# Window attention and 3x3 convolution on one core: the loops of both stages written out in line

## Chip, core and metric

The kernel runs on one core of one Trainium2 chip. The metric is the device time of one execution in microseconds. Three runs of the kernel before gave a median of 4224.94 us (4220.99 to 4227.97). The profile comes from one more execution, which took 4226.05 us by the same clock.

## What is computed

The input is x, of shape (2, 128, 256, 256) in float32. Two residual layers follow each other:

```
# layer 0: windows of 8x8 queries over 12x12 keys, 4 heads of 32
x = x + W_out * attention(W_qkv * group_norm(x))   # with relative positions and a fixed mask
# layer 1: 3x3 convolution, 128 to 128 channels, of the tile-masked input
x = x + conv3x3(tile_mask(group_norm(x))) + bias
```

The fixed mask lets each query see the keys of one parity class only. So the kernel splits the picture into four classes by the parity of row and column (PAR = 4) and runs attention with 16 queries against 36 keys.

## The kernel before, in words

Channels lie on the 128 partitions, and the 512 rows of both pictures stand one below the other. There are four phases. The first loads x, takes its statistics (VectorE) and scales the weights. A short step turns the sums into the mean and deviation of each group. The third phase is the attention stage, which writes x1 to HBM. After a second statistics step and a small table of tile masks comes the convolution stage.

**Attention.** A unit is 8 rows by half a width of 128 columns, so there are UNITS = 128. Each unit has four groups (GROUPS = 4) of four windows. In each group TensorE issues, in this order: the scores (L421, 16 products of 54 columns), half of the transposes (L401), projections q and k of a unit ahead (L386, L389), v (L434), attention times v (L451), the other half of the transposes (L401) and the output projection (L462). float32 products appear in the trace as two passes, each with its own weight load. VectorE gathers the queries of the next unit into a block layout (`sb_qb`, L541, four copies in groups 1 and 3), adds positions to the scores (L521), takes maxima and sums (L502, L506, L527), adds the output to x1 (L495) and takes the statistics of x1 (L533, L548). ScalarE evicts PSUM (L562, L566, L581, L588, L593, L599), takes the exponential (L576) and normalises the input (L610, L616). GpSimd has four kinds of elementwise operation (L635, L642, L651, L658). SyncE only issues DMAs (L348 on). The engines are coupled by counting semaphores: each instruction waits for the count that its unit and group need.

**The loop of units.** Each engine has a `body(u, s, slot, on)`, which emits what that engine does in unit u. `units(eng, body)` (L330) drives it. Units -3 to 5 are written out with constants; units 6 to 121 run in a hardware loop (L333) of 29 turns (TURNS) with four units in a turn; units 122 to 131 are written out again. A call where u is a constant emits constant waits and addresses. In the loop u is an expression of the loop's register, so that waits and the few moving addresses are computed by register instructions (`need`, L74 to L78, `settled`, L69). At the end of a turn each engine adds to its register, compares and branches back to the head of its own loop.

**Convolution.** A strip is 8 rows of 256 columns, and there are CSTRIPS = 64. The rows are combined in fours on GpSimd (L900), split into two float16 parts (L835 on ScalarE, L882 on VectorE), and 72 products of 512 columns per strip run on TensorE (L808). VectorE adds the four results (L872). ScalarE also normalises a strip ahead (L827) and starts the output with x1 plus bias (L848). `strips(eng, body)` (L753) is the same kind of driver: strips -4 to 3 in line, a loop (L756) of 14 turns (CTURNS) of four strips, the rest in line.

Of the kernel before, what the change touches and what calls it, by code (L numbers as in the profile page):

```python
# [32 lines left out]
UNITS = 2 * STRIPS  # L33
# [18 lines left out]
CSTRIPS = ROWS // CROWS  # L52
# [28 lines left out]
def conv_preact_program(nc, x_in, wqkv_in, wout_in, rel_in, wconv_in, bias_in, ident_in, gsum_in,  # L81
                        shift_in, edge_in, x1_dram, out):
    with ExitStack() as ctx:
# [205 lines left out]
        with ExitStack() as pb:  # L289
# [33 lines left out]

            FIRST, LOOP = 6, 4
            TURNS = (UNITS - 3 - FIRST) // LOOP
            GT = UNITS * GROUPS

            def units(eng, body):  # L330
                for u in range(-3, FIRST):
                    body(u, u // 2, u % 4, lambda v, top: 0 <= v < top)
                with eng.Fori(0, TURNS) as i:  # L333
                    for c in range(LOOP):
                        body(i * LOOP + (FIRST + c), i * (LOOP // 2) + (FIRST + c) // 2, (FIRST + c) % 4,
                             lambda v, top: True)
                for u in range(FIRST + LOOP * TURNS, UNITS + 4):
                    body(u, u // 2, u % 4, lambda v, top: 0 <= v < top)

            def z_at(slot, p, off, dims):  # L340
# [5 lines left out]
            @block.sync  # L346
            def _(sp):
                def body(u, s, slot, on):  # L348
                    h = slot % 2
                    if on(u + 3, UNITS):  # L350

                        row = settled(sp, (s + (h + 3) // 2) * WS)
                        need(sp, sem["zf_done"], u + 2)
                        r = (slot + 3) % 2
                        sp.dma_start(view(xb, 0, 128, r * ZR * LC, [[LC, ZR], [1, LC]]),
                                     x_in[:, bass.ds(row, ZR),
                                          (UW - PAD) * r:(UW - PAD) * r + LC]).then_inc(x_loaded[r], 16)
                    if on(u - 3, UNITS):
                        row = settled(sp, (s - 1 - (1 - h)) * WS + 1)
                        sp.wait_ge(sem["x1_done"], (u - 2) * PAR)  # L360
                        sp.dma_start(x1_dram[:, bass.ds(row, WS), UW * (1 - h):UW * (1 - h) + UW],
                                     view(x1, 0, 128, (1 - h) * WS * UW, [[UW, WS], [1, UW]])
                                     ).then_inc(sem["x1_stored"], 16)
                    if on(u - 1, UNITS):

                        row = settled(sp, (s + (h - 1) // 2) * WS + PAD)
                        done = settled(sp, (u - 2) * 16)
                        need(sp, sem["x1_read"], done)
                        need(sp, sem["x1_stored"], done)
                        r = (slot + 3) % 2  # L370
                        sp.dma_start(view(x1, 0, 128, r * WS * UW, [[UW, WS], [1, UW]]),
                                     x_in[:, bass.ds(row, WS),
                                          UW * r:UW * r + UW]).then_inc(xr_loaded[r], 16)
                units(sp, body)
                sp.wait_ge(sem["x1_stored"], UNITS * 16)

            @block.tensor
            def _(pe):
# [87 lines left out]
                def QF_BEFORE(n):  # L466
                    return min(n + PAR + 2, UNITS * PAR) if isinstance(n, int) else n + PAR + 2
                units(pe, body)

            @block.vector  # L470
            def _(dve):
# [6 lines left out]
                def body(u, s, slot, on):  # L478
                    h = slot % 2
                    for g in range(GROUPS):  # L480
# [64 lines left out]
                        if g == 2 and on(u - 3, UNITS):  # L545

                            for t, op in ((tmax, ALU.max), (tmin, ALU.min)):
                                last = dve.tensor_reduce(t[:, bass.ds((u - 3) * 4, 4)],  # L548
                                                  view(x1, 0, 128, (1 - h) * WS * UW, [[TILE, 4], [UW, WS], [1, TILE]]),
                                                  AX.XY, op)  # L550
                            last.then_inc(sem["x1_read"], 16)
                units(dve, body)

            @block.scalar
# [176 lines left out]
        with ExitStack() as pc:  # L731
# [3 lines left out]
            XR = 4  # L735
# [12 lines left out]
            ADDS = (2, 4, 5, 6)  # L748
            NADD = ADDS[-1]

            CFIRST, CTURNS = 4, 14

            def strips(eng, body):  # L753
                for j in range(-4, CFIRST):
                    body(j, j // XR, j % XR, lambda v: 0 <= v < CSTRIPS)
                with eng.Fori(0, CTURNS) as i:  # L756
                    for c in range(XR):
                        body(i * XR + (CFIRST + c), i + (CFIRST + c) // XR, (CFIRST + c) % XR, lambda v: True)
                for j in range(CFIRST + XR * CTURNS, CSTRIPS + 1):
                    body(j, j // XR, j % XR, lambda v: 0 <= v < CSTRIPS)  # L760

            block = pc.enter_context(nc.Block())
# [1 line left out]
            @block.sync  # L764
            def _(sp):
                sp.wait_ge(sem["pads"], 1)

                sp.dma_start(x1_dram[:, 0:1, :].rearrange("p a b -> p (a b)"), zrow[:]).then_inc(sem["edges"], 16)  # L768
                sp.dma_start(x1_dram[:, ROWS + 1:ROWS + 2, :].rearrange("p a b -> p (a b)"), zrow[:]
                             ).then_inc(sem["edges"], 16)  # L770
                sp.wait_ge(sem["edges"], 32)

                def body(j, t, slot, on):
                    if on(j + 4):
                        row = settled(sp, (j + 4) * CROWS)
                        need(sp, sem["zf_done"], j + 1)
                        need(sp, sem["init_done"], j + 1)
                        r = slot
                        sp.dma_start(xc[:, r * CZ * W:(r + 1) * CZ * W],
                                     x1_dram[:, bass.ds(row, CZ), :].rearrange("p a b -> p (a b)")  # L780
                                     ).then_inc(x_loaded[r], 16)
                    if on(j - 1):
                        row = settled(sp, (j - 1) * CROWS)
                        sp.wait_ge(sem["add_done"], j * NADD)
                        o = (slot - 1) % 2
                        sp.dma_start(out[:, bass.ds(row, CROWS), :].rearrange("p a b -> p (a b)"),
                                     oc[:, o * CROWS * W:(o + 1) * CROWS * W]).then_inc(stored[o], 16)
                strips(sp, body)
                for done in stored:
                    sp.wait_ge(done, CSTRIPS // 2 * 16)  # L790

            @block.tensor
            def _(pe):
                def body(j, t, slot, on):
                    if not on(j):
                        return
                    for k, m in enumerate(TERM):
                        pe.wait_ge(sem["tl_done"], j * NM + k + 1)
                        need(pe, sem["add_done"], (j - 1) * NADD + ADDS[k])
                        for half in range(2):  # L800
                            m_at = ps_c[:, (k * 2 + half) * 512:(k * 2 + half + 1) * 512]
                            c = 0
                            for kx in range(3):
                                t_at = lambda z: view(z, 0, 128, (slot % 2) * NM * TZ + k * TZ + 2 * half * CW + kx,
                                                      [[CW, 2], [1, W]])
                                tap = slice((m * 3 + kx) * C, (m * 3 + kx + 1) * C)
                                for wt, z in ((wc_h, th), (wc_h, tl), (wc_l, th)):
                                    last = pe.matmul(m_at, wt[:, tap], t_at(z), start=(c == 0), stop=(c == 8))  # L808
                                    c += 1
                        last.then_inc(sem["conv_mm"], 1)  # L810
                strips(pe, body)

            @block.scalar
            def _(act):
# [23 lines left out]
                def body(j, t, slot, on):  # L838
# [5 lines left out]
                    if on(j + 1):  # L844
# [4 lines left out]
                                       xc[:, r:r + CROWS * W], ACT.Identity, bias=bias[:, 0:1]  # L849
                                       ).then_inc(sem["init_done"], 1)  # L850
                strips(act, body)

            @block.vector
# [92 lines left out]
```

## Time and profile before

| | |
|---|---|
| median of three runs | 4224.94 us |
| profiled execution | 4226.05 us |
| its span, from the first to the last instruction | 4224.3 us |
| mean granted clock of TensorE | 0.979 |
| busy share: TensorE, VectorE, ScalarE, GpSimd | 89%, 81%, 71%, 53% |
| attention, first scores to last | 215.4 to about 3144 us |
| convolution, first product to last | 3218.7 to 4218.65 us |

In the rows PE is TensorE (PEld its weight loads), DVE VectorE, ACT ScalarE, POOL GpSimd and SP SyncE. Times are us unless marked ns. "q" behind an engine's name means its sequencer, whose register, wait and branch instructions don't count as busy. An idle time is put down to whatever ended last before it; "issue" means that the engine waited for nothing that the profile shows.

### The profile page before, as it was taken

To read this page: it belongs to the slowest core of one execution; us is meant where nothing else is said; L and a number is where in the kernel's file an instruction comes from. 1 tells how busy PE (TensorE), PEld (TensorE's weight loads), DVE (VectorE), ACT (ScalarE), POOL (GpSimd) and SP (SyncE) were. 2 spreads that over 40 slices of the span, in tenths; PEclk is the share of its full clock that TensorE was granted. 3 is DMA by queue.
4 is the path that set the end of the run, shared out by engine and by line. 5 is a ranking of instruction groups with operands and counts; after the bars stand their busy time and mean duration, and the time that the engine had idled before them with its cause. 6 is when DMAs were issued, how large, how long until landed. Compare 5 with 4: busy or idle time off the path is not lost. (4 is left out here: it accounts for less than half of the span.)

```text
span 4224.3 us, 130567 instructions
## 1 busy us (share of the span) xinstructions
PE 3778.5 (89%) x48644; PEld 2670.1 (63%) x48644; DVE 3412.0 (81%) x6126; ACT 2979.4 (71%) x5317; POOL 2257.6 (53%) x2824
## 2 busy tenths in 40 slices
PE   0099999999999999999999999999995999999999
PEld 0077777777777777777777777777772444444444
DVE  9878777778777877877787777878887988888887
ACT  0177777777777777777777777777865777777774
POOL 0055555555555555555555555555554666666664
PEclk9999999999999999999999999999997999999999
DMA  9723323233232323233232323323223433333332
GB/s 376 292 66 89 90 72 90 74 88 86 76 90 72 90 72 90 78 84 87 75 88 74 90 74 88 85 77 84 81 67 126 158 155 148 152 154 149 149 152 95
DMA packets 489962, 462.94 MB, mean 110 GB/s; under 512 B 9264, under 2 KB 468912, under 8 KB 469040
## 3 DMA queue, kind: packets, MB, share of 16 engines
q1 hardware_dynamic: 489520, 455.92, 33.3%
q8 instruction: 415, 6.80, 0.7%
q14 instruction: 27, 0.22, 0.0%
HBM read 321.40 MB, written 134.48 MB: 108 GB/s over the span
## 5 line engine op out<-in xcount | busy, mean ns | idle before, releaser
L635 POOL TENSOR_TENSOR sb_erel<-sb_brel 128x288 f32<-128x288 f32 x512 | 352.2, 688 | 902.8 <-DVE sb_brel L502 902.7
L900 POOL TENSOR_TENSOR sb_tf<-sb_cf 128x1024 f32<-128x1024 f32 x256 | 609.7, 2383 | 391.9 <-DVE sb_tl L882 370.4
L421 PEld LDWEIGHTS ps_s<-sb_kf,sb_qb 128*64 128x64 f32 x16384 | 532.8, 140 | 351.1 <-issue 333.6
L421 PE MATMUL ps_s<-sb_kf,sb_qb 128*64 128x54 f32 x16384 | 599.7, 228 | 172.1 <-issue 113.6
L651 POOL TENSOR_TENSOR sb_prod<-sb_rel,sb_shift 128x192 f32<-128x192 f32 x1024 | 596.7, 603 | 200.3 <-DVE sb_rel L511 200.3
L401 PE MATMUL ps_t<-sb_ident,sb_d 128*108 128x128 f32 x4096 | 674.5, 288 | 1.0 <-ACT sb_pt L599 1.0
L541 DVE COPY sb_qb<-sb_qf 32x512 f32<-32x512 f32 x1024 | 636.8, 622 | 25.7 <-ACT sb_qf L562 15.4
L808 PE MATMUL ps_c<-sb_th,sb_wc_h 128*128 128x512 f16 x1536 | 584.7, 381 | 39.6 <-DVE sb_tl L882 39.6
L434 PEld LDWEIGHTS ps_v<-sb_wq,sb_zf 128*108 128x108 f32 x4096 | 516.1, 174 | 158.7 <-issue 88.6
L808 PE MATMUL ps_c<-sb_th,sb_wc_l 128*128 128x512 f16 x1536 | 583.6, 380 | 0.0
L808 PE MATMUL ps_c<-sb_tl,sb_wc_h 128*128 128x512 f16 x1536 | 583.5, 380 | 0.0
L642 POOL TENSOR_TENSOR sb_d<-sb_scores,sb_srcp 128x288 f32<-128x288 f32 x512 | 343.3, 671 | 392.9 <-DVE sb_srcp L517 385.1
L581 ACT COPY sb_pt<-ps_t 108x512 f32<-108x512 f32 x512 | 297.4, 581 | 347.1 <-PE ps_t L401 347.1
L434 PE MATMUL ps_v<-sb_wq,sb_zf 128*108 128x128 f32 x4096 | 533.4, 273 | 0.0
L401 PEld LDWEIGHTS ps_t<-sb_ident,sb_d 128*108 128x108 f32 x4096 | 418.1, 133 | 80.2 <-issue 2.1
L835 ACT CAST sb_th<-sb_tf 128x1024 f16<-128x1024 f32 x256 | 264.0, 1043 | 259.4 <-POOL sb_tf L900 259.4
L495 DVE SCALAR_TENSOR_TENSOR sb_x<-ps_q,sb_oscale,sb_x 128x256 f32<-128x256 f32 x512 | 247.4, 483 | 243.2 <-PE ps_q L462 235.0
L389 PE MATMUL ps_k<-sb_zf,sb_wq 128*128 128x396 f32 x1024 | 435.9, 507 | 0.3 <-ACT sb_kf L566 0.3
L882 DVE TENSOR_TENSOR sb_tl<-sb_tf,sb_th 128x1024 f16<-128x1024 f32 x256 | 408.1, 1594 | 19.9 <-ACT sb_th L835 19.9
L566 ACT COPY sb_kf<-ps_k 128x576 f32<-128x576 f32 x512 | 329.7, 644 | 123.8 <-PE ps_k L389 110.9
L872 DVE SCALAR_TENSOR_TENSOR sb_oc<-ps_c,sb_wscale,sb_oc 128x1024 f32<-128x1024 f32 x256 | 322.6, 1281 | 94.3 <-PE ps_c L808 94.3
L506 DVE TENSOR_REDUCE sb_ssum<-sb_scores 128x8 f32<-128x288 f32 x512 | 230.7, 451 | 205.8 <-ACT sb_scores L576 193.0
(96 smaller groups left out, 6725.1 us busy)
## 6 DMA issues: line engine op xcount, KB each, us to landing
sb_xb<-rows SPq DMA_DIRECT2D x128, 780.0 KB, 6.6
sb_xc<-x SPq DMA_DIRECT2D x64, 1280.0 KB, 5.3
sb_abuf<-rows SPq DMA_DIRECT2D x32, 2048.0 KB, 10.9
sb_x<-rows SPq DMA_DIRECT2D x128, 512.0 KB, 3.9
x<-sb_x SPq DMA_DIRECT2D x128, 512.0 KB, 3.8
out<-sb_oc SPq DMA_DIRECT2D x64, 1024.0 KB, 3.8
sb_raw<-wconv SPq DMA_DIRECT2D x1, 576.0 KB, 3.8
x<-sb_zrow SPq DMA_DIRECT2D x2, 128.0 KB, 1.7
```

The source lines that it names most:

```text
L389: pe.matmul(ps_k[:, 0:PLANE], wq[:, C:2 * C], z_at(slot, p, 0, [[1, PLANE]]), start=True, stop=True).then_inc(sem["k_mm"], 1)
L401: last = pe.transpose(ps_t[0:KV, wj * 128:(wj + 1) * 128], d[:, at:at + KV], ident[:])
L421: last = pe.matmul(s_at, qb[:, qc:qc + QB], kf[:, kc:kc + KR], start=True, stop=True)
L434: last = pe.matmul(ps_v[0:KV, p * C:(p + 1) * C], z_at(vslot, p, GW * WK * vg, [[1, KV]]), wq[:, 2 * C:3 * C], start=True, stop=True)
L541: last = dve.tensor_copy(view(qb, DH * hd, DH * hd + DH, (1 - h) * QBW + p0 * NW * QB + hd * QN, [[QB, 2 * NW], [1, QN]]), view(qf, DH * h ...
L566: act.copy(view(kf, 0, 128, vh * KU + p * NW * KR, [[KR, NW], [1, KN]]), view(ps_k, 0, 128, 0, [[WK, NW], [1, KN]])).then_inc(sem["kf_done ...
L635: pool.tensor_tensor(view(erel, 0, 128, 0, [[KN, PAIRS], [KS, KS], [1, KS]]), view(brel, 0, 128, 0, [[KS, PAIRS], [0, KS], [1, KS]]), view ...
L642: pool.tensor_tensor(view(d, 0, 128, b0 * DB, [[DSLOT, PAIRS], [1, KN]]), view(sp_, 0, 128, b0 * NS, [[KN, PAIRS], [1, KN]]), view(srcp, 0 ...
L651: last = pool.tensor_tensor(view(prod, 0, 128, ax * PAIRS * KS * QS, [[KS * QS, PAIRS], [QS, KS], [1, QS]]), view(rel, 0, 128, b0 * PAIRS ...
L808: last = pe.matmul(m_at, wt[:, tap], t_at(z), start=(c == 0), stop=(c == 8))
L882: dve.tensor_tensor(view(tl, 0, 128, at, [[CW, PAIRROWS], [1, W]]), view(tf, 0, 128, k * TF, [[W, PAIRROWS], [1, W]]), view(th, 0, 128, at ...
L900: pool.tensor_tensor(tf[:, k * TF:(k + 1) * TF], view(cf, 0, 128, c0 + ra * W, [[2 * W, PAIRROWS], [1, W]]), view(cf, 0, 128, c0 + rb * W, ...
```

## The change

Both drivers lose their loop. Every unit and every strip is emitted in line, by the call that was used before for the first and the last of them, so that all waits and addresses are constants. The bodies, the order of work, the semaphores and the buffers stay as they are. The loops of the first phase (L220, L270) stay too.

```diff
             GT = UNITS * GROUPS
-            FIRST, LOOP = 6, 4
-            TURNS = (UNITS - 3 - FIRST) // LOOP
 
             def units(eng, body):
-                for u in range(-3, FIRST):
-                    body(u, u // 2, u % 4, lambda v, top: 0 <= v < top)
-                with eng.Fori(0, TURNS) as i:
-                    for c in range(LOOP):
-                        body(i * LOOP + (FIRST + c), i * (LOOP // 2) + (FIRST + c) // 2, (FIRST + c) % 4,
-                             lambda v, top: True)
-                for u in range(FIRST + LOOP * TURNS, UNITS + 4):
+                for u in range(-3, UNITS + 4):
                     body(u, u // 2, u % 4, lambda v, top: 0 <= v < top)
...
-            CFIRST, CTURNS = 4, 14
-
             def strips(eng, body):
-                for j in range(-4, CFIRST):
-                    body(j, j // XR, j % XR, lambda v: 0 <= v < CSTRIPS)
-                with eng.Fori(0, CTURNS) as i:
-                    for c in range(XR):
-                        body(i * XR + (CFIRST + c), i + (CFIRST + c) // XR, (CFIRST + c) % XR, lambda v: True)
-                for j in range(CFIRST + XR * CTURNS, CSTRIPS + 1):
+                for j in range(-4, CSTRIPS + 1):
                     body(j, j // XR, j % XR, lambda v: 0 <= v < CSTRIPS)
```

## Rows read from the trace of the kernel before

**Rows 1.** The page: busy time and the DMA queues (packets, MB, share of 16 engines)

```profile
PE 3778.5 (89%) x48644; PEld 2670.1 (63%) x48644; DVE 3412.0 (81%) x6126; ACT 2979.4 (71%) x5317; POOL 2257.6 (53%) x2824
...
q8 instruction: 415, 6.80, 0.7%
```

**Rows 2.** Chain that ended last, in order of time: start, us, what

```profile
3218.70 999.95 PE ps_c L808 x4608
```

**Rows 3.** Waits of PE from 343 to 3022 us: total, times, longest

```profile
PE ps_s L421 <- issue: 113.6, 28, 5.2
PE ps_s L421 <- DVE sb_qb L541: 45.8, 88, 0.5
```

**Rows 4.** Line L333, the attention loop's own instructions: count, ns min/median/max, first and last start

```profile
L333 DVEq COMPARE_BRANCH  x29: 50/56/80, 427.1 to 3019.0; - x29
...
L333 PEldq COMPARE_BRANCH  x29: 76/4480/5847, 428.3 to 3020.3; - x29
L333 ACTq COMPARE_BRANCH  x29: 40/45/45, 429.0 to 3020.9; - x29
```

**Rows 5.** Line L756, the convolution loop's branch on PE, same columns

```profile
L756 PEldq COMPARE_BRANCH  x14: 76/208/237, 3341.7 to 4152.3; - x14
```

**Rows 6.** Stretches: length, busy and instructions of PE, PEld, DVE, ACT, POOL, then PEclk, DMA, GB/s

```profile
342.59:433.09 90.50, 85.00 (x1376) 68.05 (x1377) 74.30 (x163) 70.08 (x132) 52.04 (x81) 1.00 0.33 91
433.09:525.39 92.30, 86.71 (x1377) 69.23 (x1377) 73.09 (x160) 70.17 (x132) 51.35 (x80) 0.98 0.30 82
...
386.24:408.04 21.80, 21.24 (x344) 17.01 (x345) 18.26 (x41) 17.50 (x34) 12.85 (x20) 1.00 0.31 86
...
433.09:456.59 23.50, 22.93 (x345) 18.19 (x345) 16.96 (x38) 17.47 (x33) 12.14 (x19) 0.93 0.18 47
298.50:320.45 21.95, 21.30 (x345) 17.00 (x345) 18.62 (x41) 17.48 (x33) 12.43 (x20) 1.00 0.31 87
3043.67:3065.63 21.96, 21.31 (x344) 17.00 (x344) 18.58 (x41) 17.48 (x33) 12.44 (x20) 1.00 0.31 88
...
3218.70:4218.60 999.90, 999.90 (x4608) 450.77 (x4608) 862.84 (x638) 721.61 (x1070) 603.88 (x254) 1.00 0.37 145
```

**Rows 7.** PE in order of time: first scores of units 6, 10 and 122 (start, us)

```profile
342.59 1.14 PE L421 MATMUL ps_s<-sb_kf,sb_qb 128*64 128x54 f32 x32 [0.85 <-DVE sb_qb L541]
...
433.09 1.14 PE L421 MATMUL ps_s<-sb_kf,sb_qb 128*64 128x54 f32 x32 [3.75 <-issue]
...
3021.71 1.14 PE L421 MATMUL ps_s<-sb_kf,sb_qb 128*64 128x54 f32 x32 [0.44 <-DVE sb_qb L541]
```

**Rows 8.** Waits of PE, longest first, 205 to 340 us, then 3022 to 3150 us

```profile
PE ps_s L421 <- DVE sb_qb L541: 5.7, 5, 2.6
PE ps_q L386 <- ACT sb_zf L616: 2.8, 2, 2.4
PE ps_s L421 <- DVE sb_scores L521: 2.5, 1, 2.5
...
PE ps_s L421 <- DVE sb_qb L541: 3.6, 5, 1.0
PE ps_t L401 <- ACT sb_pt L599: 0.3, 1, 0.3
```

**Rows 9.** DVE and POOL in order of time, first in unit 4 (in line), then in unit 8 (loop)

```profile
307.26 2.67 DVE L541 COPY sb_qb<-sb_qf 32x512 f32<-32x512 f32 x4
307.24 1.17 POOL L651 TENSOR_TENSOR sb_prod<-sb_rel,sb_shift 128x192 f32<-128x192 f32 x2
...
395.00 2.52 DVE L541 COPY sb_qb<-sb_qf 32x512 f32<-32x512 f32 x4
395.06 1.37 POOL L651 TENSOR_TENSOR sb_prod<-sb_rel,sb_shift 128x192 f32<-128x192 f32 x2
```

**Rows 10.** Code fetches (queue q8) from 203 to 342 us, then from 433 to 3022 us

```profile
q8 instruction: 15, 0.25, 0.7%
...
q8 instruction: 363, 5.95, 1.0%
```

## The prediction

> **What bounds the kernel now.** I read the page first, then the waits of TensorE, then the driver loops' own lines, and last the length of single units. TensorE is the busiest engine with 89% of the span [rows 1], and the convolution stage is TensorE from end to end: 4608 products back to back in 999.95 us [rows 2], 217 ns each, at full clock [rows 6]. Nothing that the other engines do there can shorten it. In attention TensorE idles little, and from 343 to 3022 us its waits have two names only [rows 3]: 28 pauses before the first scores of a unit with the releaser "issue", 113.6 us together and up to 5.2 us each, and 88 waits of about 0.5 us for VectorE's gather of the queries (`sb_qb`).
>
> Those counts are those of the loop. It has 29 turns of four units, so 28 jumps back and 3 x 29 + 1 = 88 other unit starts. The loop's own line settles it: TensorE's branch takes 4480 ns in the median (76 ns in the one case that must be the last turn, where it falls through), while the same branch takes 45 ns on ScalarE and 56 ns on VectorE [rows 4]. In the convolution loop TensorE's branch takes 208 ns [rows 5], hidden under the queue of products already issued.
>
> **Why only there.** A turn of the attention loop holds 1376 products and 1377 weight loads of TensorE [rows 6], over 2750 instructions; a convolution turn holds 4 x 72 x 2 = 576. The long turn pays at its jump, the short one does not. The code queue moved 363 packets of 16.4 KB from 433 to 3022 us, 13 per turn, so code is fetched anew in each turn [rows 10]. The Trainium skill (Runtime: NRT & Kernel Launch, Instruction fetch mechanics) says that code is prefetched in sequence only, that TensorE holds 2048 instructions, and that a taken branch outside what is held stops the engine for a fetch. By that rule the trace agrees, 4.48 us against 0.21 us.
>
> **The change, term by term.** The sum is made on the profiled execution (4226.05 us, span 4224.3, 1.1 us above the median of the runs).
>
> *Attention, units 6 to 121.* The first scores of unit 6 start at 342.59 us and those of unit 122 at 3021.71 us [rows 7]: 2679.12 us for 116 units. What do 116 units take without a jump? There are two rows for it. A unit inside a turn takes 21.80 to 21.84 us, of which I take 21.83; a unit that is already in line takes 21.95 or 21.96 us [rows 6], of which I take 21.96.
>
> Taken apart: a full turn is 92.30 us against 4 x 21.83 = 87.32, so a jump costs 5.0 us in a typical turn. The pause gives 3.2 of it (3.75 us of idle at 433.09, less the 0.5 us that TensorE waits for VectorE at any unit start). The other 1.7 us is the clock: the unit behind the jump takes 23.50 us at a granted clock of 0.93, where others have 1.00 and 21.83 [rows 6]. TensorE has been idle for 3.75 us before it, and for a part of the unit it is granted 1.2 GHz, the lower of its two levels. Over the loop the jumps cost 2679.12 - 116 x 21.83 = 146.8 us. All of it goes if no jump is left.
>
> Given back: a unit in line is 0.13 us longer. It comes from the four copies of L541, which take 2.67 us in line and 2.52 us in the loop [rows 9], and TensorE waits for the last of them at each unit start. In the loop GpSimd's sequencer computes its wait values between the operations (L78), which I take to be why its two L651 fall otherwise against the copies: in line they run 1.17 us instead of 1.37, and the copies beside them are the longer ones. I see that shift in both stretches in line, at the start and at the end, with the same 18.6 us of VectorE per unit against 18.3 [rows 6]. So I take 21.96 for all: 116 x 0.13 = 15.1 us back. Net 146.8 - 15.1 = **131.7 us** gained. The bound below is 131.7, the bound above 146.8 if the loop's rhythm could be kept.
>
> *Register work.* It all goes. On TensorE, VectorE and GpSimd what it was worth inside a unit is already in the 0.13 us, with its sign against the change. On SyncE it could only let DMAs start earlier, and TensorE has no DMA among its waits in the loop [rows 3]; the cover is the unit or more by which loads run ahead, and were it gone, L610 and L495 would be late next.
>
> *Convolution.* Zero. The 64 strips take 15.6 us each (999.95 / 64), in line and in the loop alike, since the products are back to back [rows 2].
>
> *Code fetches that are new.* The convolution loop on TensorE holds its code, and in line it must be fetched. An instruction is at most 68 B (13 packets of 16.4 KB over the 3129 products, loads and operations of a turn [rows 6, 10]), so its 2 x 4608 are 38 packets, beside 145 GB/s of data (0.37 of the DMA engines) where attention has some 85 (0.31) [rows 6]. The other engines' bodies too stream now in both stages. Where a packet comes in time it costs nothing; where it comes late, the nearest price is a jump's, 3.2 to 5.0 us. In the two attention stretches in line TensorE has no wait called "issue" at all [rows 8], though 15 packets came before 342 us [rows 10]. That row is nearest, so I take 0; the other end, 38 x 5.0 = 190 us, goes to a rival.
>
> *Edges.* The start of attention, its last units and both statistics steps are in line already and stay as they are.
>
> Sum: 4226.05 - 131.7 = 4094.3 for an execution like the profiled one, 4093 against the median.
>
> **Rivals.**
>
> *1. The loop's rhythm survives (gain 147).* The 0.13 us hangs on the moments at which GpSimd starts against VectorE; a phase settled over 120 units could fall as in the loop. Then 4224.9 - 147 = 4078. For it: the copies' time is fickle (2.52 or 2.67). Against it: units at the start and at the end, reached from different histories, agree within 0.01 us [rows 6]. Chance 0.14.
>
> *2. A few late packets.* Some of the roughly 380 packets (13 per four units, 116 units) of attention arrive late, in a unit where a large load holds the DMA engines. Five of them at 5.0 us make 4118. Chance 0.05.
>
> *3. Slower: TensorE's code comes late in the convolution.* There no slack exists, each pause adds in full, and clock goes with it. If each of the 38 new packets stopped TensorE by 5.0 us, 190 - 132 = +58, so 4283. It decides from 27 late packets on (132 / 5.0 = 26.4). For it: the loop there held its code, so that fetching under that DMA load is shown only by the few strips in line. Against it: a strip of 15.6 us needs 0.6 of a packet (38 / 64), and eight strips in line show no gap [rows 2]. Chance 0.02.
>
> *4. The change does not remove what it should.* The pause at the turn's end might be something else than the jump (a wait that both forms have). The branch rows of the other engines, 29 x 50 ns, would then be the price: 1.5 us, so 4223. Against it: the pause is absent at all unit starts in line. Chance 0.01. The Trainium skill (Advanced Engine Details and Errata, Control Flow Timing) speaks for this one: it gives about 108 ns for a compare-and-branch, by which all 43 branches of TensorE would be worth an estimated 4.6 us and the result would be 4220. The 4480 ns of the row decide against it.
>
> **How the numbers follow.** The forecast has 0.78, the rivals 0.14, 0.05, 0.02 and 0.01. The predicted time is 4093 us. The range goes down to rival 1 with some 2 us for the run to run spread of the median, 4076, and up to a few late packets, 4110. About 0.2% (8 us) is what a measurement of this kernel can tell from no change. Faster by more: 0.78 + 0.14 + 0.05 = 0.97, less a little for what I did not think of, 0.96; the same 0.02; slower 0.02.
>
> **What would show it.** In the profile after: no branch of 4 us in attention and no "issue" wait of TensorE before L421; unit starts 21.96 us apart throughout, with VectorE's `sb_qb` ahead of each by 0.65 us and copies of 2.67 us; the clock at 1.00 from about 220 us to the end of attention, its mean near 0.98 or above; the first scores of unit 122 at about 2890 us; convolution still 999.95 us of L808 without a gap; more code packets than 415, mostly in the convolution. Wrong it would be if unit lengths scatter (late packets), if TensorE shows "issue" gaps in L808, or if the units in line take 21.83 or something new beyond 22 us.

## The result

The changed kernel takes 4093.9 us in the median of four runs (4092.59 to 4094.01), the kernel before 4222.97 us (4218.44 to 4227.97). The ratio is 0.9693, with a 95% interval from 0.9677 to 0.971. The forecast was 4093 in a range from 4076 to 4110. The profiled execution is one with 4093.9 us and a span of 4092.0 us; its sum in the forecast was 4094.3.

**The profile after.** Busy time and code queues, from the page of the changed kernel; they answer to [rows 1]:

```profile
PE 3734.7 (91%) x48644; PEld 2630.7 (64%) x48644; DVE 3459.8 (85%) x6126; ACT 2971.6 (73%) x5317; POOL 2210.9 (54%) x2824
...
q8 instruction: 389, 6.37, 0.6%
q14 instruction: 169, 1.38, 0.1%
```

Every engine executes as many operations as before, and TensorE is busy 44 us less: its products run at full clock where some of them had run at half. VectorE is busy 48 us more for the same 6126 operations; 33 of them are the gather's copies (L541 636.8 us before, L533 669.7 us after). Both differences matter below.

All that TensorE waits for from 343 to 2889 us, against [rows 3]:

```profile
PE ps_s L413 <- DVE sb_qb L533: 75.8, 115, 0.7
```

The 28 pauses called "issue" are gone. Every unit start now waits for VectorE's gather, 0.66 us each (75.8 / 115), where it was 0.52 in the loop (45.8 / 88).

TensorE in order of time, the first scores of units 6 and 122, against [rows 7]; then stretches of those 116 units, of one unit in the middle and of the convolution, against [rows 6] (columns as there); then the code packets in the convolution:

```profile
342.51 0.27 PE L413 MATMUL ps_s<-sb_kf,sb_qb 128*64 128x54 f32 x2 [0.66 <-DVE sb_qb L533]
...
2889.24 0.38 PE L413 MATMUL ps_s<-sb_kf,sb_qb 128*64 128x54 f32 x5 [0.66 <-DVE sb_qb L533]
...
342.51:2889.24 2546.73, 2470.32 (x39904) 1972.62 (x39904) 2156.66 (x4641) 2026.43 (x3828) 1442.62 (x2320) 1.00 0.32 87
...
1528.01:1549.96 21.95, 21.29 (x345) 17.00 (x345) 18.59 (x41) 17.48 (x33) 12.44 (x20) 1.00 0.32 86
3086.91:4086.41 999.50, 999.46 (x4608) 450.50 (x4608) 873.76 (x638) 721.65 (x1070) 604.09 (x254) 1.00 0.38 146
...
q8 instruction: 37, 0.61, 0.2%
```

Units 6 to 121 take 2546.73 us in place of 2679.12. That is 132.4 us less, at 21.954 us per unit (2546.73 / 116), with the clock at 1.00 throughout. The spans differ by 132.3 us (4224.3 less 4092.0), so attention explains all of it. The convolution takes 999.5 us as before, although 37 packets of TensorE's code (queue q8) now arrive in it, where 7 did before.

### The profile page after: what moved, and what is told of

Same layout as the page of the kernel before. It is cut to its first block and busy times, and to the rows that moved or that the text cites. A ratio compares the mean times of both kernels' runs of the same rounds, so it can differ in the third digit from the quotient of the medians.

```text
span 4092.0 us, 121981 instructions
## 1 busy us (share of the span) xinstructions
PE 3734.7 (91%) x48644; PEld 2630.7 (64%) x48644; DVE 3459.8 (85%) x6126; ACT 2971.6 (73%) x5317; POOL 2210.9 (54%) x2824
## 5 line engine op out<-in xcount | busy, mean ns | idle before, releaser
L627 POOL TENSOR_TENSOR sb_erel<-sb_brel 128x288 f32<-128x288 f32 x512 | 352.4, 688 | 997.9 <-DVE sb_brel L494 997.8
L413 PEld LDWEIGHTS ps_s<-sb_kf,sb_qb 128*64 128x64 f32 x16384 | 519.9, 138 | 268.6 <-DVE sb_qb L533 137.1
L533 DVE COPY sb_qb<-sb_qf 32x512 f32<-32x512 f32 x1024 | 669.7, 654 | 25.6 <-ACT sb_qf L554 15.3
L413 PE MATMUL ps_s<-sb_kf,sb_qb 128*64 128x54 f32 x16384 | 586.4, 225 | 89.0 <-DVE sb_qb L533 86.4
L393 PE MATMUL ps_t<-sb_ident,sb_d 128*108 128x128 f32 x4096 | 662.4, 284 | 1.0 <-ACT sb_pt L591 1.0
L643 POOL TENSOR_TENSOR sb_prod<-sb_rel,sb_shift 128x192 f32<-128x192 f32 x1024 | 549.7, 558 | 200.2 <-DVE sb_rel L503 200.2
L867 DVE TENSOR_TENSOR sb_tl<-sb_tf,sb_th 128x1024 f16<-128x1024 f32 x256 | 419.4, 1638 | 20.1 <-ACT sb_th L820 20.0
L381 PE MATMUL ps_k<-sb_zf,sb_wq 128*128 128x396 f32 x1024 | 425.0, 496 | 0.3 <-ACT sb_kf L558 0.3
L650 POOL TENSOR_TENSOR sb_scores<-sb_scores,sb_smax 128x288 f32<-128x288 f32 x512 | 388.4, 759 | 0.2 <-DVE sb_smax L519 0.2
```

Of the source, the lines that this page charges most:

```text
L381: pe.matmul(ps_k[:, 0:PLANE], wq[:, C:2 * C], z_at(slot, p, 0, [[1, PLANE]]), start=True, stop=True).then_inc(sem["k_mm"], 1)
L393: last = pe.transpose(ps_t[0:KV, wj * 128:(wj + 1) * 128], d[:, at:at + KV], ident[:])
L413: last = pe.matmul(s_at, qb[:, qc:qc + QB], kf[:, kc:kc + KR], start=True, stop=True)
L533: last = dve.tensor_copy(view(qb, DH * hd, DH * hd + DH, (1 - h) * QBW + p0 * NW * QB + hd * QN, [[QB, 2 * NW], [1, QN]]), view(qf, DH * h ...
L627: pool.tensor_tensor(view(erel, 0, 128, 0, [[KN, PAIRS], [KS, KS], [1, KS]]), view(brel, 0, 128, 0, [[KS, PAIRS], [0, KS], [1, KS]]), view ...
L643: last = pool.tensor_tensor(view(prod, 0, 128, ax * PAIRS * KS * QS, [[KS * QS, PAIRS], [QS, KS], [1, QS]]), view(rel, 0, 128, b0 * PAIRS ...
```

## The experiments

Four kernels split the change by engine, four change the loop's length, leave products out or change the convolution alone, and two put GpSimd a little later. `units` got an argument for this: an engine runs its units either in the old loop or in line.

```diff
-            def units(eng, body):
-                for u in range(-3, UNITS + 4):
-                    body(u, u // 2, u % 4, lambda v, top: 0 <= v < top)
+            def units(eng, body, loop=False):
+                if not loop:
+                    for u in range(-3, UNITS + 4):
+                        body(u, u // 2, u % 4, lambda v, top: 0 <= v < top)
+                    return
+                for u in range(-3, FIRST):
...
-                units(pe, body)
+                units(pe, body, loop=True)
```

### Where the loss sits: one engine in line, or one in the loop

**TensorE in line, the other four in the loop** (`loop=True` for sp, dve, act, pool). Expected:

> Attention: TensorE in line, the other four engines in the old loop of units; convolution in line. Theory (the jump of TensorE is the whole loss, the 0.13 us per unit given back comes from the other engines' code in line): no pause, all units at 21.83 us, 116 x 0.12 = 15 us under the changed kernel, about 4079. Rival (the other engines' jumps carry part of the loss): the unit behind a jump stays longer than 21.83 and the time is above 4094. Rival for the 0.13 us (it belongs to TensorE's own code in line): 21.95 us per unit, 4094.

**TensorE in the loop, the other four in line.** Expected:

> Attention: only TensorE in the old loop, the other four in line; convolution in line. Theory: 28 pauses of 3.7 to 5.2 us stay, each jump costs 5.0 us, and units take 21.95 us between them: 4094 + 28 x 5.0 = 4234, a little more than the kernel before. Rival (the loss needs all engines' jumps): below 4200.

They took 4061.71 and 4257.24 us; the kernel before took 4228.98 us beside them. The long waits of TensorE at the scores, first with TensorE in line, then with TensorE in the loop:

```profile
PE ps_s L426 <- DVE sb_qb L546: 67.7, 127, 1.1
```

```profile
PE ps_s L426 <- issue: 106.3, 28, 5.5
PE ps_s L426 <- DVE sb_qb L546: 66.9, 99, 1.1
```

Only TensorE's own jumps pause it. With the other four still looping there is no pause, and with them in line all 28 stay. That part of the expectation held. The sizes did not: the first kernel's units take 21.70 us, not 21.83, and the second one's 22.12 us, not 21.95 (a stretch of one unit of each, columns as in [rows 6]):

```profile
1511.95:1533.65 21.70, 21.19 (x344) 16.97 (x344) 18.22 (x41) 17.54 (x34) 12.81 (x20) 1.00 0.32 88
```

```profile
1603.25:1625.37 22.12, 21.41 (x345) 17.01 (x345) 18.64 (x41) 17.56 (x33) 12.41 (x20) 1.00 0.31 86
```

So two things of opposite sign hide in the 0.13 us per unit by which units in line are longer than units in the loop. One of them is TensorE's own register work (some 19 register instructions in a unit of the loop, none in line), which costs about 0.15 us per unit: 21.83 against 21.70 with the other engines looping, 22.12 against 21.95 with them in line. Over 116 units the 0.17 us are 20 of the 23 us by which the second kernel lies above the expected 4234.

**Only GpSimd in the loop**, then **only VectorE in the loop**. Expected:

> Attention: only GpSimd in the old loop, the rest in line; convolution in line. Theory (GpSimd's register work between its operations is what shortens VectorE's copies of L541 from 2.67 to 2.52 us): units at 21.83 us, about 4079. Rival (it is VectorE's or ScalarE's own register work): units stay at 21.95 us, 4094.

> Attention: only VectorE in the old loop, the rest in line; convolution in line. Theory (the 0.13 us is GpSimd's): units stay at 21.95 us, 4094. Rival (it is VectorE's own register work): 21.83 us, 4079.

They took 4064.22 and 4091.81 us. A unit with only VectorE in the loop:

```profile
1525.75:1547.71 21.96, 21.30 (x345) 17.00 (x345) 18.56 (x41) 17.50 (x33) 12.43 (x20) 1.00 0.31 86
```

The other part is thus GpSimd's: its loop alone brings units from 21.95 to 21.70 us (in the median; 21.83 was expected), as much as the loops of all four engines did, while VectorE's does nothing (21.96 us). VectorE's gather and GpSimd's products beside it, in order of time, first in the changed kernel, then with GpSimd in the loop:

```profile
1536.77 2.67 DVE L533 COPY sb_qb<-sb_qf 32x512 f32<-32x512 f32 x4
1536.75 1.16 POOL L643 TENSOR_TENSOR sb_prod<-sb_rel,sb_shift 128x192 f32<-128x192 f32 x2
```

```profile
1522.68 2.53 DVE L546 COPY sb_qb<-sb_qf 32x512 f32<-32x512 f32 x4
1522.74 1.37 POOL L656 TENSOR_TENSOR sb_prod<-sb_rel,sb_shift 128x192 f32<-128x192 f32 x2
```

In the changed kernel GpSimd starts 0.02 us ahead of VectorE, and VectorE's four copies take 2.67 us. With GpSimd looping it starts 0.06 us behind, the copies take 2.53 us, and GpSimd's two products pay for it (1.37 against 1.16 us), which costs nothing since GpSimd waits for VectorE anyway (997.8 us in 509 waits in the changed kernel). There are two gathers in a unit, so VectorE saves 0.28 us of which 0.25 reaches the unit.

### Is it register work or the delay it makes?

Both of the next kernels are in line everywhere and have one short operation more on GpSimd:

```diff
                             need(pool, sem["b_done"], n)
+                            if g % 2 == 1:
+                                pool.memset(pspare[:], 0.0)
                             for ax in range(2):
```

with `g % 2 == 0` in the second. Expected:

> The changed kernel, all in line, with one more operation on GpSimd: a memset of one column ahead of the first L643 in groups 1 and 3, where VectorE gathers the queries. Theory (who starts first at the gather decides: the changed kernel's first product of L643 starts 0.02 us before VectorE's first copy, which then takes 0.77 us instead of 0.41): the memset puts GpSimd some 0.1 us later, the four copies take 2.52 us, units 21.70 us, and the time is about 4064 without any register work. Rival (register work in GpSimd's sequencer does something else than delay): units 21.95 us or more, 4094.

> The same memset, in groups 0 and 2, where VectorE has no gather. Theory (only the order at the gather matters): copies 2.67 us, units 21.95 us, 4094, as the changed kernel. Rival (any delay on GpSimd shifts the rhythm of the unit): something near 21.70 us and 4064.

The first took 4061.95 us (median of four, 4061.27 to 4062.27), a ratio of 0.961 to the kernel before with an interval from 0.9594 to 0.9626. The second took 4097.97 us. A unit, the gather and GpSimd beside it, with the memset in groups 1 and 3:

```profile
1511.27:1532.98 21.71, 21.20 (x344) 16.99 (x345) 18.25 (x41) 17.56 (x34) 12.99 (x22) 1.00 0.33 90
...
1520.06 2.53 DVE L534 COPY sb_qb<-sb_qf 32x512 f32<-32x512 f32 x4
1520.02 0.10 POOL L643 MEMSET sb_pspare<- 128x1 f32 x1
1520.07 1.42 POOL L646 TENSOR_TENSOR sb_prod<-sb_rel,sb_shift 128x192 f32<-128x192 f32 x2
```

and with the memset in groups 0 and 2, where nothing is gathered:

```profile
1541.61 2.67 DVE L534 COPY sb_qb<-sb_qf 32x512 f32<-32x512 f32 x4
1541.58 1.17 POOL L646 TENSOR_TENSOR sb_prod<-sb_rel,sb_shift 128x192 f32<-128x192 f32 x2
```

The memset takes 0.10 us. In groups 1 and 3 it puts GpSimd's first product 0.01 us behind the start of VectorE's first copy, in place of 0.02 us ahead, and this gives the whole 0.25 us per unit without any register work; in groups 0 and 2 it gives none (median unit 21.95 us). Which of the two starts first at the gather decides, the copy or the product; the memset itself starts ahead of the copy and does no harm. The traces show it in nearly all of the 256 gathers: behind a product that starts 0.02 us ahead the first copy takes 0.77 us (changed kernel), with the product 0.01 us behind it takes 0.41 us (memset kernel). By what mechanism the first to start holds up the other is not shown here.

The second kernel is 4 us above the changed one for another reason, at its first products:

```profile
224.89 0.97 POOL L646 TENSOR_TENSOR sb_prod<-sb_rel,sb_shift 128x192 f32<-128x192 f32 x2 [7.14 <-issue]
```

GpSimd stands for 7.14 us once, in unit 0, and TensorE behind it. GpSimd's configuration instructions ahead of the first product, in this kernel and in the changed one (count, ns min/median/max, first and last start), point at why:

```profile
L646 POOLq MODIFY_POOL_CONFIG  x2: 11/11/11, 217.8 to 217.8; - x2
```

```profile
L643 POOLq MODIFY_POOL_CONFIG  x2: 11/11/11, 193.9 to 193.9; - x2
```

In the changed kernel they run at 193.9 us and the first product follows at 217.9 us, so that whatever they start has 24 us. Here the memset of group 0 comes first and waits for VectorE (`sb_rel`), and they come behind it, at 217.8 us, 7.1 us before the product. That the pause is theirs fits these rows; no run tests it.

The kernel with TensorE in line and the other engines looping, the memset kernel and the changed one were timed on one chip. Expected of the other two:

> Timed: attention with TensorE in line and the other four engines in the loop, convolution in line. Both theories that are left say units of 21.70 us and about 4062, some 32 us under the changed kernel.

> The changed kernel on the same chip as the runs beside it: 4094 within 3.

The changed kernel took 4093.15 us (4091.86 to 4093.26) there, TensorE in line with the others looping 4063.41 us (4062.71 to 4063.63; ratio 0.9613, interval 0.9597 to 0.9629), and the memset version 4061.95 us. The last is the fastest of them, 31.2 us below the changed kernel.

### Why a jump costs TensorE 5 us

**Twice the turn** (LOOP = 8 in place of 4, every engine, convolution in its loop). Expected:

> The kernel before with a turn of 8 units in the attention loop instead of 4 (14 turns, 13 jumps), all engines, and the convolution in its old loop. Theory (a jump costs 5.0 us each time, pause 3.2 and clock 1.7, whatever the length of a turn that is longer than what TensorE holds): 13 pauses, 4223 - 15 x 5.0 = 4148. Rival (the pause grows with the code jumped over): pauses of twice the length, 4223 within 15.

It took 4156.06 us, with the kernel before at 4235.05 us beside it. Waits of TensorE, the stretches of a unit behind a jump and of units 6 to 121, then the code packets from 342 to 2951 us:

```profile
PE ps_s L426 <- DVE sb_qb L546: 64.2, 114, 2.6
PE ps_s L426 <- issue: 51.3, 13, 5.0
...
519.54:543.87 24.33, 23.77 (x344) 18.95 (x345) 18.26 (x41) 17.99 (x34) 12.83 (x20) 0.89 0.25 68
341.49:2951.40 2609.91, 2499.17 (x39904) 1999.70 (x39904) 2122.68 (x4641) 2031.62 (x3828) 1485.75 (x2320) 0.98 0.31 85
...
q8 instruction: 345, 5.65, 0.9%
```

The pause is 3.9 us (51.3 / 13) against 4.1 before (113.6 / 28), so it does not grow with the code jumped over. Units 6 to 121 take 2609.91 us, 77.6 above 116 x 21.83, for 13 jumps, where 28 jumps cost 146.8. That is 6.0 us for a jump against 5.2; over 13 jumps it makes about the 8 us by which the time came out above the expected 4148. The difference is clock: the unit behind the jump shown takes 24.33 us at a granted clock of 0.89, the one in [rows 6] 23.50 us at 0.93. The pause is the same, the stretch at 1.2 GHz behind it is longer. A longer turn is not needed for that. The units behind all jumps take 24.37 us in the mean here (23.12 to 24.75) and 23.55 us in the kernel before (23.22 to 24.66), but 24.21 us with TensorE alone in the loop, whose turn is of four units as well. What decides it stays open.

**What the pause waits for.** The trace has the start and end of each code packet. In the pause of [rows 7] (the branch starts at 428.32 us) queue q8 moves one packet from 428.32 to 432.7 us:

```profile
q8 instruction: 1, 0.02, 1.6%
```

In all 28 pauses of the kernel before, a packet of TensorE's code starts 1.6 to 3.4 us after the branch does, and the branch ends 1.35 to 1.54 us after that packet has landed. So the pause is as long as the packet is late: 4.1 us of branch for the earliest, 5.7 us for the latest. TensorE waits for code at its jump; that this packet holds the code at the target is the plain reading of it, the trace does not say what is in a packet.

**Fewer instructions in the same turn.** Two kernels shorten TensorE's work: the scores take 8 products over 128 rows in place of 16 over 64, and attention times v takes 4 in place of 16. The results of attention are others then, so only the jumps are read, not the time against the kernel before.

```diff
-                                for px in range(2):
+                                for px in range(1):
...
-                                for hd in range(HEADS):
-                                    o_at = ps_o[DH * hd:DH * hd + DH, par * 512 + p * 64:par * 512 + (p + 1) * 64]
+                                for hd in range(1):
+                                    o_at = ps_o[:, par * 512 + p * 64:par * 512 + (p + 1) * 64]
```

> The kernel before with fewer products: the scores take 8 products of 128 rows in place of 16 of 64 (wrong queries), attention times v takes 4 of 128 rows in place of 16 of 32 (all heads with the first head's probabilities). A turn of four units then has 368 x 4 = 1472 TensorE instructions in place of 2752. Theory (a jump stops TensorE only where the turn is longer than the code that it holds, and 1472 fit as 576 do in the convolution): TensorE's branch takes about 0.2 us, no pauses called issue, no extra code packets, unit starts evenly apart. Rival (any jump in attention stops TensorE, because it waits for its queue to empty): branches of 4 us and 28 pauses as before.

> As the run with fewer products, but with a turn of 8 units, so 2944 TensorE instructions in a turn. Theory (length of the turn decides): branches of over 4 us again, 13 of them, and code packets in every turn; the time is longer than that of the run with four units by up to 13 x 5 = 65 us, less what other engines' work hides since TensorE is no longer the bound. Rival (not the length): as with four units.

The attention loop's branch on TensorE (count, ns min/median/max), with turns of four units, then of eight, and for the latter the code packets from 500 to 3000 us:

```profile
L338 PEldq COMPARE_BRANCH  x29: 76/208/229, 447.6 to 3121.8; - x29
```

```profile
L338 PEldq COMPARE_BRANCH  x14: 79/5192/6575, 542.2 to 3111.5; - x14
...
q8 instruction: 183, 3.00, 0.5%
q14 instruction: 154, 1.26, 0.2%
```

With 1472 instructions in a turn the branch takes 208 ns, as in the convolution's loop [rows 5], TensorE has no wait called "issue", and neither code queue moves anything in the stretch. With 2944 the branch takes 5192 ns, 13 pauses are back (48.0 us) and so is the code: 183 packets. The other engines' code is fetched anew as well (q14), yet their branches stay at 45 to 63 ns. The times are 4351.78 and 4427.96 us. The difference is 76 us, over the 65 that were called the most: TensorE is still the busiest engine here (92% and more), so other engines' work hides little of a jump. The length of the turn decides; what TensorE can hold lies between 1472 and 2752 products and weight loads (1601 and 2881 with its register, wait and branch instructions). The Trainium skill (Runtime: NRT & Kernel Launch, Instruction fetch mechanics) gives 2048, and the two runs agree with it.

**The convolution alone in line**, attention in its loop. Expected:

> Convolution in line, attention in its old loop on all engines. Theory (the convolution is worth nothing, and its new code packets cost nothing): 4223 within 3, convolution products back to back in 999.9 us. Rival (late code packets under the convolution's DMA load): gaps at L808 and a time above 4230.

It took 4226.78 us (the kernel before 4235.05 on that chip, and 4226.14 in the median of seven runs on another), with 114.0 us in 28 pauses in attention. The convolution's products, from the chain that ended last:

```profile
3218.90 1000.47 PE ps_c L806 x4608
```

They run back to back, in 1000.47 us against 999.95. So the convolution's half of the change is worth nothing that these runs can tell, and its code comes in time. The time is 0.8 us outside the 4223 within 3 that was expected, and within the spread of the kernel before (4218.44 to 4235.05); the rival, above 4230 with gaps, did not show.

## Why the prediction was right

*The pause and its place.* Right. The 28 pauses belong to TensorE's jumps alone, since four looping engines beside TensorE in line make none, and they come from the turn's length, since 1472 instructions make none and 2944 do. In the kernel before, the branch ends 1.35 to 1.54 us after a packet of TensorE's code has landed, in each of the 28.

*146.8 us for the jumps.* Right in sum, and its parts hold: the pause is 3.9 to 4.1 us, of which 0.5 is a wait for VectorE that any unit has, the rest is clock. In the changed kernel the clock stays at 1.00 over all 116 units. That the clock part is no constant (1.7 us in the turn shown, 24.33 - 21.83 = 2.5 with turns of eight) was not foreseen and does not matter here.

*21.96 us per unit in line.* Right: 21.954. The units in line of the kernel before, of which [rows 6] show two, were enough to read the length of 116 more. This row decided the forecast between 4093 and 4078.

*The reason for the 0.13 us.* Half right. The step "given back: a unit in line is 0.13 us longer", from the copies of L541, named the right operations, and the run with GpSimd alone in the loop and the one with the memset show it. But the term is a net of two: 0.25 us lost at VectorE's gather, and 0.13 us won because TensorE's register work goes. The forecast did not suffer, since the units in line that it was read from hold both parts. The text let the copies' difference (0.15 us, at two gathers per unit 0.30) stand beside 0.13 without asking where the rest was. For that reason rival 1, "the loop's rhythm survives", was sized at 4078; with the rhythm and TensorE in line together the time is 4062, below the range given.

*Rivals 2 to 4.* No late packets in attention (its only wait is for VectorE), none in the convolution under its load of 146 GB/s, and the branch was what was paid.

*Code packets.* "More code packets than 415" was wrong in direction for the queue that it counts, q8, which fell to 389; q14 rose from 27 to 169. The step took the 13 packets per turn for all engines' code. But q8 carries TensorE's alone: with the other four engines looping it stays at 389 while q14 falls to 45. From 433 to 3022 us q8 moved 363 packets, 13 per turn, while a turn's units in line need fewer: 319 from 343 to 2889 us, 11 for four units. With turns of eight (345 packets from 342 to 2951 us) a turn moves 24, so four units take 11 in the loop too, and the other two go with the jump. The 38 expected for TensorE in the convolution were 37. None of it touches the time.

*The register work on TensorE* was said to be "already in the 0.13 us, with its sign against the change". It was in it, but with its sign for the change: 0.13 to 0.17 us per unit.

## What to carry to other kernels

A hardware loop whose turn is longer than what TensorE can hold pays at each jump, here 5 to 6 us of pause and lowered clock: either keep a turn under that length, or write out TensorE's part alone. Here the other engines could go on looping at no cost. Where a kernel has units both in a loop and in line, compare their lengths before and apart from the jumps: the difference is what constants and registers are worth, with its sign. When two engines start within 0.1 us of each other again and again, as VectorE and GpSimd do here, try a tiny shift of the one that has time to spare: here it was worth more than the work it added.

## What was not expected

- The order of two starts 0.02 us apart is worth 0.14 us at each gather: four copies take 2.67 us when GpSimd is first and 2.53 us when VectorE is.
- One memset of 0.10 us on GpSimd, 256 times, makes the kernel 31 us faster.
- The lower clock behind a pause of the same length lasts longer in some turns than in others: in the kernel before the unit behind a jump takes from 23.22 to 24.66 us.
- A jump to code that TensorE no longer holds also moves about two packets more than the turn has, and TensorE's branch ends some 1.4 us after the first packet behind it has landed.
